# A graph network on one core: the four output additions of a turn of layer 1 moved into one block of VectorE's loop

## What is computed

```python
x_u = data @ var_u                      # 8 logits of a node
x_v = data @ -var_u
logits = x_u[edge_src] + x_v[edge_dst] + var_c
q = softmax(logits, axis=-1)            # 8 heads
x_sep = data[edge_dst] * edge_vals[:, None]
for m in range(8):
    agg = segment_sum(q[:, m:m+1] * x_sep, edge_src, num_segments=3125)
    y = y + agg @ var_w[m]
return y + var_b
```

## Time and profile before

| what | value |
|---|---|
| time, median of 3 runs | 2374.38 us (2373.89 to 2381.76) |
| the profiled execution, its own time | 2375.3 us |
| its span in the trace | 2373.6 us |
| layer 1's loop and its tail | about 1220 to 2360 us of the span |
| busy in the span | PE 72%, DVE 60%, POOL 68%, ACT 23% |
| TensorE's granted clock | 0.90 of full speed in 0 to 1150 us, 0.51 in 1220 to 2360 us |

### The profile page before, as it was taken

The page is one execution under the profiler, slowest core; times in us unless marked ns, Lnnn a source line. Parts: engine busy times, 40 slices in busy tenths (PEclk is TensorE's granted clock), DMA queues, the critical chain, the costliest instruction groups (busy, mean ns, idle before and its releaser), DMA issues.

```text
span 2373.6 us, 53585 instructions
## 1 busy us (share of the span) xinstructions
PE 1700.9 (72%) x10041; PEld 1192.6 (50%) x10041; DVE 1422.4 (60%) x6161; ACT 555.3 (23%) x1979; POOL 1625.3 (68%) x1700
## 2 busy tenths in 40 slices
PE   5698888899899989989845555555655555565554
PEld 5455555555555555556434444444444444444444
DVE  5334434444434444343358888788888888888885
ACT  2233333333333333332111111111111111111110
POOL 2777777777777777774456766667676766767673
PEclk7799999988989898898555555555555555555555
DMA  2544444444444444442133333333333333333332
GB/s 68 120 99 100 96 97 99 98 94 96 100 93 102 98 98 95 96 103 52 38 109 90 94 90 93 89 91 93 91 92 92 92 90 90 94 90 92 92 91 57
DMA packets 353203, 216.99 MB, mean 91 GB/s; under 512 B 284700, under 2 KB 325751, under 8 KB 352926
## 3 DMA queue, kind: packets, MB, share of 16 engines
q0 software_dynamic: 66800, 113.26, 21.0%
q1 hardware_dynamic: 284692, 102.18, 17.9%
q10 hardware_dynamic: 1684, 1.24, 0.2%
HBM read 209.80 MB, written 6.69 MB: 91 GB/s over the span
## 4 chain that ended last, share of the span: by engine, by line
DVE 28%; issue 25%; POOL 17%; PE 16%; DVEq 7%; DMA 6%; ACT 1%; POOLq 0%; SPq 0%; ACTq 0%
POOL X L581 16%; DMA X<-table_src,slot_s 4%; DVE EQW L1134 4%; DVE EQW L1140 3%; DVEq L1199 3%; PE bank L1363 3%; PE bank L1346 2%; DVE EX L1180 2%; DVE OT L976 2%; DVE r L1172 2%; DVE r L1176 2%; PE bank L1372 2%; DVE r L1167 2%; PE bank L1354 2%; DVE OE L1185 2%
## 5 line engine op out<-in xcount | busy, mean ns | idle before, releaser
L589 POOL DMA_INDIRECT G<-table_node_and_list,slot_s x825 | 796.1, 965 | 378.5 <-issue 210.6
L581 POOL DMA_INDIRECT X<-table_src,slot_s x825 | 789.6, 957 | 295.3 <-issue 234.4
L1482 PE MATMUL bank<-Q,G 125*64 125x128 f32 x1650 | 414.9, 424 | 183.6 <-DVE Q L1193 183.6
L1482 PEld LDWEIGHTS bank<-Q,G 125*64 125x64 f32 x1650 | 313.7, 221 | 196.4 <-issue 125.9
L1346 PE MATMUL bank<-filler 128*128 128x384 bf16 x1100 | 377.1, 343 | 1.6 <-issue 1.6
L990 DVE TENSOR_TENSOR sT<-sT,bank 65x16 f32 x275 | 46.2, 168 | 551.7 <-PE bank L1382 513.6
L1493 PE MATMUL bank<-R,w_z 65*64 65x64 f32 x1104 | 133.9, 316 | 278.2 <-DVE sT L1201 278.2
L976 DVE TENSOR_SCALAR OT<-KBT,base_p 48x375 bf16<-48x375 int32 x550 | 231.7, 422 | 65.6 <-issue 35.2
L1493 PEld LDWEIGHTS bank<-R,w_z 65*64 65x64 f32 x1104 | 122.9, 224 | 282.5 <-issue 281.2
L1363 PE MATMUL bank<-XT,w_ex 128*64 128x375 f32 x550 | 254.3, 547 | 7.5 <-issue 7.5
L1372 PEld LDWEIGHTS bank<-w,H 65*125 65x125 f32 x1650 | 232.3, 200 | 0.0
(11 more groups left out here) (168 smaller groups left out, 2072.5 us busy)
## 6 DMA issues: line engine op xcount, KB each, us to landing
KBT<-in_dst SPq DMA_DIRECT2D x550, 70.3 KB, 2.1
X<-in_edge_attr SPq DMA_DIRECT2D x275, 93.8 KB
HK<-keys SPq DMA_DIRECT2D x275, 93.8 KB
X<-table_src,slot_s POOLq DMA_INDIRECT x825
G<-table_node_and_list,slot_s POOLq DMA_INDIRECT x825
BW<-table_dst_parts SPq DMA_DIRECT2D x275, 6.0 KB
UW<-table_logit_src_parts SPq DMA_DIRECT2D x275, 0.8 KB, 1.7
table_node_and_list<-sm SPq DMA_DIRECT2D x1, 1562.5 KB
```

The costliest lines, as they stand in the source:

```text
L581: pool.indirect_dma_start(X[:, j, q, D:2 * D], None, tA, bass.IndirectOffsetOnAxis(ap=slot_s[:, j, q:q + 1], axis=0)).then_inc(gat_a[0][j] ...
L589: pool.indirect_dma_start(G[:, j, q, :], None, tH, bass.IndirectOffsetOnAxis(ap=slot_s[:, j, q:q + 1], axis=0)).then_inc(g_gather[j], 16)
L1482: last = pe.matmul(bank[2 + j % 2][0:D, 0:WM], G[0:P, j, q, 0:D], Q[:, j % 2, q].rearrange("p m n -> p (m n)"), start=(q == 0), stop=(q == ...
```

## The change

`add_outputs` is called in the bodies with j = 0 only, at the end of the body instead of near its start. It waits for the turn's product, reads the four addresses with four `value_load` one after the other, and then makes the four additions, each behind its wait for the one before. The additions of turn t now all stand in VectorE's body 4t + 8. For the last turn, which has three groups, there are three.

```diff
             def add_outputs(t, j):
+                own = [j for j in range(RB) if not isinstance(t, int) or RB * t + j < NG]
                 dve.wait_ge(u_y, t + 1)
-                done(dve, u_acc, t, j, 1)
-                first = dve.value_load(first_of[0:1, bass.ds(RB * t + j, 1)], min_val=0, max_val=N - WG)
-                to = yT[:, bass.ds(first, WG)]
-                dve.tensor_tensor(to, to, bank[6][0:D, j * WG:(j + 1) * WG], ALU.add).then_inc(u_acc, 1)
+                firsts = [dve.value_load(first_of[0:1, bass.ds(RB * t + j, 1)], min_val=0, max_val=N - WG) for j in own]
+                for j, first in zip(own, firsts):
+                    done(dve, u_acc, t, j, 1)
+                    to = yT[:, bass.ds(first, WG)]
+                    dve.tensor_tensor(to, to, bank[6][0:D, j * WG:(j + 1) * WG], ALU.add).then_inc(u_acc, 1)
@@
                 back(window_places, t, j, 2)
-                back(add_outputs, t, j, 2 * RB)
                 back(exp_sums, t, j, 2)
@@
                 back(reverse_sums, t, j, 1)
                 back(logits_less_max, t, j, 1)
+                if j == 0:
+                    back(add_outputs, t, j, 2 * RB)
```

## The result

The changed kernel takes **2465.03 us** (median of 4 runs, 2461.24 to 2476.86) against 2374.14 us before (4 runs, 2370.86 to 2381.76). The ratio is 1.039, with a 95% interval of 1.0352 to 1.0427: 91 us slower. I had forecast 2484 us and slower. The profiled execution took 2463.45 us and its span is 2461.6 us, 88.0 us longer than before's. The chip has a second, slower state, and all medians here leave out the two executions that fell into it, 3420.70 us of the run with the read under L1140 and 2513.16 us, the profiled one, of the run without the check where the read is partly covered.

What follows compares the result with a forecast made beforehand. VectorE's own stream was taken to bound layer 1: 3.73 us added less 2.13 saved is +1.60 us a turn, +109 us over 68 turns on 2375.3, giving 2484 us. Likeliest case's range 2450 to 2515; 8-in-10 range 2412 to 2515.

Steps and rivals of the forecast that it cites:

- the likeliest case: Four reads in layer 1 run in series, net +1.60 us a turn: 2484 us, chance 0.73.
- VectorE bounds layer 1, TensorE's wait costs nothing: Layer 1: VectorE's own stream sets the time; removing the product's 4.2 us wait once a turn gains next to nothing.
- The price of a read, 0.71 us in series: VectorE's sequencer: address step, load, check and assertion take 0.71 us a read, one read behind the other.
- The block, 3.73 us: End of the j = 0 body: four reads and four additions move L976 from 0.56 to 4.29 us behind L1144.
- The savings, 2.13 us: Between L1185 and L1163 in four bodies: without read and addition, 0.40 + 0.54 + 0.40 + 0.79 us a turn.
- The last turn, nothing: Last turn's three additions stand in bodies with little else; no cost or saving was counted.
- Rival 4, the exponential at the loop boundary: ScalarE's exponential still holds L1163 there, saving 0.39 not 0.79 us: 2511 us; no own chance, inside the 0.73.
- The figure of the Trainium skill: About 200 ns a register load would make four reads 0.42 us shorter: net 1.18 us a turn, 2456 us.
- the cover: Ahead of the block: only L1144 and L1158 cover the reads, contained in the 0.56 us between L1144 and L976.

Runs made afterwards that it cites:

- the read under L1140: Kernel before, with read and addition one a body placed between L1154 and L1144, in bodies 4t+7 to 4t+10: 2398.54 us, ratio 1.0106.
- the run without the check where the read is partly covered: Kernel before, each addition one body earlier and its read without the bounds check: 2292.86 us, ratio 0.9658.
- the first experiment: Kernel before, each addition one body earlier, reads unchanged, so TensorE's product no longer waits: 2363.73 us, ratio 0.996.
- the three at about 2305 us: Changed kernel without reads, 2304.28 us; kernel before with read under L1134 and addition parted, 2307.46 us; the latter without bounds check, 2308.01 us.

## Why the prediction was right

The time lies 19 us below the forecast and inside the likeliest case's own range of 2450 to 2515 us. By its steps:

- **VectorE bounds layer 1, TensorE's wait costs nothing**: shown. Its removal alone brings 10 us, the whole change loses 91.
- **The price of a read, 0.71 us in series**: shown by the loads' starts in the block, and by the runs without checks (0.43 us apart) and without reads.
- **The block, 3.73 us**: 4.21 - 0.56 = 3.65 us. The additions are 0.30 us apart and not 0.31, and L976 follows the last by 0.24.
- **The savings, 2.13 us**: with 0.12 us and not 0.10 from L1185 to L1163 they are 2.05 us by the same distances. The two errors cancel: 3.65 - 2.05 = 1.60 us, what I had forecast.
- **The term that was missing**: the mean turn grew by 1.38 us, from 16.62 to 18.00 (1.42 us by the turn that I had read). The 0.22 us between is in neither place. Waits for a gather, 1.6 us in 1000 before, are 0.03 of it; the rest are small steps between L1163 and L1134 that have grown shorter in the changed kernel. More than half also comes when only the product's wait goes (16.50 against 16.62 us a turn, reads untouched), so that part has to do with when TensorE works; the rest stays open. In 68 turns it is 15 us, most of the miss of 21 us against the profiled execution.
- **"The last turn, nothing"**: from the last L976 to the last L1163 it takes 6.9 us (2429.1 to 2436.0) and was 9.9 (2338.6 to 2348.5). These 3 us are not the reads: the first experiment keeps them in these bodies and takes 7.4 us (2324.6 to 2332.0). They are two waits for a gather there, 2.48 and 0.25 us, that only the kernel before has:

```profile
2346.78 0.36 DVE L1134 TENSOR_TENSOR EQW<-G,key_back 125x192 f32<-125x192 f32 x1 [2.48 <-DMA G<-table_node_and_list,slot_s]
```

Another 3 us lie ahead of layer 1's first L1163, which starts at 1207.9 instead of 1211.0 us; no edit accounts for them.
- **Rival 4, the exponential at the loop boundary**: the case does not exist. I had read its end, 0.50 us behind L1185, as a second bound. The first experiment moved it ahead and L1163 did not move.
- **The figure of the Trainium skill** (page "Runtime: NRT & Kernel Launch", section "Instruction fetch mechanics", about 200 ns a register load): its estimate of 2456 us is nearer to the measured time than mine, by chance. The loads took 0.297 to 0.317 us, and the missing microseconds were elsewhere. Its words "even for bulk" hold: each of four loads in a row paid in full.

What the prediction had right by luck as much as by reasoning is the cover. It gave the block only L1144 and L1158 because the sequencer waits at L1144; my first attempt to use this the other way round (the read under L1140) missed by 119 us.

## What to carry to other kernels

A register read in the stream of the engine that bounds the kernel is paid by what it finds running. Put it directly behind a long instruction and ahead of the next one with an open wait; do not gather such reads: here they ran in series and only the first found cover. A long wait on an engine that is idle 43% of the time, like TensorE's 4.2 us here, is no gain to be had until someone is shown to wait behind it. And where the bounds are sure, the check is worth leaving out: it is 0.28 of the 0.71 us, 71 and 75 us of the whole in two kernels, and nothing where GpSimd already held the turn.

## What the runs showed of the hardware

A load of one integer from the core's own memory held VectorE's sequencer for 0.30 us, with or without a second one behind it, and the comparison step of the check for 0.19 us.

The sequencer stood still at vector instructions whose semaphore waits were open, although no record of the sequencer shows these waits. The Trainium skill, page "Perfetto Trace Analysis", section "DVE / Act Engine Instruction (TENSOR_ADD, Activation, etc)", has the instruction pushed into a wait queue, after which the sequencer is ready for the next. The rows of the read under L1140 agree with that for one waiting instruction at most: with L1140's wait open, the read two places behind it did not begin.

GpSimd's gathers differ in length from kernel to kernel: 964 ns in the mean before (1300 to 2300 us), 980 ns in the kernel of 2293 us, 999 to 1002 ns in the three at about 2305 us, and 1046 ns with the read under L1140, whose VectorE is less busy than before's. So it is not how busy VectorE is that decides. In the last, one of 1.30 us starts at 1802.31, 0.08 us behind L1193, and the same recurs in most bodies (171 of over 1.2 us in 236 bodies). I did not test what the two share.
